# Perceiver layer on one core: the opening by row tile, a sixth key projection in the first block, and the first pair's sums taken from PSUM

## The reference

```python
x = x + xattn(layernorm(x), ctx, Wq, bq, Wk, bk, Wv, bv, Wo, bo)   # 16 heads of 32
x = x + attn(layernorm(x), ...)                                     # self attention, top 128
x = x + ffn(layernorm(x), ...)                                      # 8 experts, top 2

def xattn(q_in, kv, ...):
    q, k, v = heads(q_in @ Wq.T + bq), heads(kv @ Wk.T + bk), heads(kv @ Wv.T + bv)
    return merge(softmax(q @ k.T * 32**-0.5) @ v) @ Wo.T + bo
```

## Time and profile before

| | |
|---|---|
| median of 3 runs | 1579.67 us (1578.26 to 1581.8) |
| span of the profiled execution, first to last instruction | 1576.5 us |
| median less span | 3.2 us |
| time of the profiled execution itself | not recorded beside the three runs; only its span is |
| PE busy | 1508.9 us, 96% of the span |
| DVE, ACT, POOL busy | 79%, 65%, 26% |
| mean granted TensorE clock | 0.981 of full speed |
| PE busy in the first of 40 slices | 6 tenths |
| block 1 | to about 46.9 us |
| block 2 | 46.9 to about 564 us |

### The profile page before, as it was taken

The page is one execution under the profiler, slowest core; times in us unless marked ns, Lnnn a source line. Parts: engine busy times, 40 slices in busy tenths (PEclk is TensorE's granted clock), DMA queues, the critical chain, the costliest instruction groups (busy, mean ns, idle before and its releaser), DMA issues. The chain is left out here.

```text
span 1576.5 us, 23638 instructions
## 1 busy us (share of the span) xinstructions
PE 1508.9 (96%) x8658; PEld 869.0 (55%) x8658; DVE 1240.5 (79%) x1876; ACT 1021.3 (65%) x1343; POOL 411.2 (26%) x225
## 2 busy tenths in 40 slices
PE   6899999999999999999999999999999965999998
PEld 4566666666666554444443444444445732799995
DVE  6877676776767869999998999999876878476664
ACT  3466666666666768888888888888726941244441
POOL 5564545636447010502100400100004420100002
PEclk9999999999999999999999999999999987899999
DMA  6354444444444455456646444545247045399994
GB/s 234 131 189 141 174 174 142 179 153 167 165 157 160 126 142 129 120 129 189 158 114 153 114 127 114 127 114 128 61 54 161 2 159 223 127 340 349 360 333 140
DMA packets 119777, 254.57 MB, mean 161 GB/s; under 512 B 10152, under 2 KB 26536, under 8 KB 115184
## 3 DMA queue, kind: packets, MB, share of 16 engines
q1 hardware_dynamic: 117632, 248.35, 51.1%
q0 software_dynamic: 1408, 4.46, 0.9%
q10 hardware_dynamic: 624, 0.27, 0.1%
HBM read 182.26 MB, written 61.34 MB: 155 GB/s over the span
## 5 line engine op out<-in xcount | busy, mean ns | idle before, releaser
L800 ACT ACTIVATE att_pr<-b_sc 128x1024 f32<-128x1024 f32 x512 | 479.9, 1037 | 82.9 <-PE b_sc L700 82.2
L850 DVE TENSOR_TENSOR att_tot<-att_tot,att_pr 128x2048 f32<-128x2048 f32 x184 | 427.3, 2322 | 21.6 <-ACT att_pr L800 3.4
L519 DVE CUSTOM_DVE_ANT_0 ctx_size<-ctx_tot,ctx_size 128x512 f32<-128x512 f32 x512 | 333.0, 688 | 127.2 <-PE ctx_tot L430 124.1
L481 ACT ACTIVATE ctx_size<-ctx_dif 128x1024 f32<-128x1024 f32 x256 | 262.5, 1025 | 120.0 <-PE ctx_dif L430 120.0
L700 PE MATMUL b_sc<-g_stacks,att_kst 98*128 98x512 f32 x1024 | 298.5, 422 | 1.9 <-DMA att_kst<-keys_scratch 1.7
L700 PEld LDWEIGHTS b_sc<-g_stacks,att_kst 98*128 98x128 f32 x1024 | 174.7, 189 | 192.2 <-ACT att_pr L800 143.2
L714 PE MATMUL b_o<-att_pr,att_val 128*32 128x512 f32 x2048 | 258.4, 602 | 0.9 <-issue 0.9
L430 PE MATMUL ctx_dif<-ctx_k_dif,f_q_hi 32*128 32x512 f32 x512 | 128.2, 497 | 5.8 <-DVE ctx_best L519 4.5
L430 PE MATMUL ctx_tot<-ctx_k_sum,f_q_hi 32*128 32x512 f32 x512 | 127.8, 497 | 0.0
L86 PE MATMUL f_proj<-f_wv_hi,g_stacks 128*128 128x512 f32 x320 | 120.5, 420 | 0.0
L86 PE MATMUL f_proj<-g_stacks,f_wk_hi 128*128 128x512 f32 x352 | 119.4, 420 | 0.3 <-DVE f_k_lo L211 0.3
(11 more groups left out here) (314 smaller groups left out, 2177.2 us busy)
## 6 DMA issues: line engine op xcount, KB each, us to landing
m_w<-in_W SPq DMA_DIRECT2D x30, 2048.0 KB, 10.1
att_kst<-keys_scratch SPq DMA_DIRECT2D x192, 256.0 KB, 4.0
f_raw<-in_ctx SPq DMA_DIRECT2D x32, 1024.0 KB, 6.0
keys_scratch<-f_k_hi SPq DMA_DIRECT2D x32, 512.0 KB, 2.8
keys_scratch<-f_k_lo SPq DMA_DIRECT2D x32, 512.0 KB, 3.2
values_scratch<-ctx_v SPq DMA_DIRECT2D x32, 512.0 KB, 3.4
att_val<-values_scratch SPq DMA_DIRECT2D x64, 256.0 KB, 2.7
rows_scratch<-mix_blank SPq DMA_DIRECT2D x1, 3840.0 KB, 24.1
```

The source lines that it names most:

```text
L481: act.activation(size[:, i % ABS, :], dif[:, :], ACT.Abs).then_inc(s_size, 1)
L519: dve.tensor_tensor_reduce(out=size[:, i % ABS, r * CH:(r + 1) * CH], in0=tot[i % 2][:, r * CH:(r + 1) * CH], in1=size[:, i % ABS, r * CH: ...
L800: act.activation(pr[:, T % SLOTS, 2 * s:2 * s + 2, :], sc[(2 * T + s) % PAIRS][:, :].rearrange("p (j q) -> p j q", j=2), ACT.Exp, scale=SC ...
L850: dve.tensor_tensor(tot[b % 2][:, :, :], so_far, pr[:, T % SLOTS, :, :], ALU.add).then_inc(s_add, 1)
```

## The change

Block 1: x arrives in four DMAs, tiles 0 and 2 issued by SP ahead of the weights and 1 and 3 by ACT ahead of the biases, each with its own semaphore. DVE aggregates tile t-1 behind the statistics of tile t. PE makes 12 products with the identity as soon as that exists, then transposes tile by tile as each tile of h is there (all four columns of one tile into one bank), and ACT copies a bank to a strided quarter of `hT`. At the end PE makes output 5 in place of the ten `keep_warm` matmuls, once `k_lo` of output 3 is done.

Block 2: output 5 is gone from PE's list. `first_pair` now computes (bank + bias) - k_hi[0] and (bank + bias) + k_hi[0] from the PSUM bank that holds the chunk 1 keys, and it stands ahead of the `k_lo` of its output.

```diff
-            sp.dma_start(c.x[:, :, :], c.dram["x"].rearrange("(t p) d -> p t d", p=P)).then_inc(x_in, 16)
+            for t in range(0, NT, 2):
+                sp.dma_start(c.x[:, t, :], c.dram["x"][P * t:P * t + P, :]).then_inc(x_in[t], 16)
...
+            for t in range(1, NT, 2):
+                act.dma_start(c.x[:, t, :], c.dram["x"][P * t:P * t + P, :]).then_inc(x_in[t], 16)
...
-            for k in range(DC):
-                act.wait_ge(s_tp, k + 1)
-                act.activation(hT[:, k, :], tp[k % 2][:, :], ACT.Copy).then_inc(s_hT, 1)
+            for t in range(NT):
+                act.wait_ge(s_tp, t + 1)
+                act.activation(hT[:, :, t * P:(t + 1) * P], tp[t % 2][:, :].rearrange("p (k q) -> p k q", k=DC),
+                               ACT.Copy).then_inc(s_hT, 1)
...
-            pe.wait_ge(s_h, NT)
-            for k in range(DC):
-                if k >= 2:
-                    pe.wait_ge(s_hT, k - 1)
-                for t in range(NT):
-                    mm = pe.transpose(tp[k % 2][:, t * P:(t + 1) * P], h[:, t, k * P:(k + 1) * P], c.ident[:, :])
+            keep_warm(pe, tp[0][:, 0:P], c.ident[:, :], c.ident[:, :], 12)
+            for t in range(NT):
+                pe.wait_ge(s_h, t + 1)
+                if t >= 2:
+                    pe.wait_ge(s_hT, t - 1)
+                for k in range(DC):
+                    mm = pe.transpose(tp[t % 2][:, k * P:(k + 1) * P], h[:, t, k * P:(k + 1) * P], c.ident[:, :])
                 mm.then_inc(s_tp, 1)
...
-            keep_warm(pe, tp[0][:, :], c.wk_hi[:, 0, 0:P], c.wk_hi[:, 0, :], 10)
+            pe.wait_ge(c.k_lo_done, G)
+            split_product(pe, c.proj[1][:, :], [(c.wk_hi[:, k, P:2 * P], c.wk_lo[:, k, P:2 * P]) for k in range(DC)],
+                          [(c.hi[1][:, k, :], c.lo[1][:, k, :]) for k in range(DC)]).then_inc(c.s_out, 1)
...
-    for t in range(NT):
-        dve.bn_stats(stats[:, t, :], x[:, t, :]).then_inc(s_stats, 1)
-    for t in range(NT):
-        dve.wait_ge(s_stats, t + 1)
-        dve.bn_aggr(mv[:, t, :], stats[:, t, :]).then_inc(s_stats, 1)
+    for t in range(NT + 1):
+        if t < NT:
+            dve.wait_ge(x_in[t], 16)
+            dve.bn_stats(stats[:, t, :], x[:, t, :]).then_inc(s_stats, 1)
+        if t:
+            dve.wait_ge(s_stats, max(2 * t - 2, 1) if t < NT else 2 * NT - 1)
+            dve.bn_aggr(mv[:, t - 1, :], stats[:, t - 1, :]).then_inc(s_stats, 1)
...
-            project(FIRST - 1, 0, WHOLE)
             pe.wait_ge(s_pair0, 2)
...
+                    if n == 1:
+                        first_pair(at)
                     dve.wait_ge(k_hi_done, count("k", o + 1))
                     dve.scalar_tensor_tensor(out=k_lo[:, at, :], in0=proj[o % 2][:, :], scalar=c.bk[:, at:at + 1],
                                              in1=f32(k_hi[n % 2][:, at, :]), op0=ALU.add, op1=ALU.subtract).then_inc(k_lo_done, 1)
-                    if n == 1:
-                        first_pair(at)
 
             def first_pair(at):
-                even, odd = f32(k_hi[0][:, at, :]), f32(k_hi[1][:, at, :])
-                dve.tensor_tensor(k_dif[0][:, at, :], even, odd, ALU.subtract).then_inc(s_pair0, 1)
-                dve.tensor_tensor(k_sum[0][:, at, :], even, odd, ALU.add).then_inc(s_pair0, 1)
+
+                o = KT + at
+                dve.wait_ge(k_hi_done, o + 1)
+                for out, op in ((k_dif, ALU.subtract), (k_sum, ALU.add)):
+                    dve.scalar_tensor_tensor(out=out[0][:, at, :], in0=proj[o % 2][:, :], scalar=c.bk[:, at:at + 1],
+                                             in1=f32(k_hi[0][:, at, :]), op0=ALU.add, op1=op).then_inc(s_pair0, 1)
```

More of the change, by code:

```diff
@@ L132, in prepare @@
         qp = [pb(f"qp{i}", [P, N]) for i in range(2)]
-        x_in, wq_in, wk_in, wv_in, small_in = (sem(n) for n in ("x_in", "wq_in", "wk_in", "wv_in", "small_in"))
+        x_in = [sem(f"x_in{t}") for t in range(NT)]
+        wq_in, wk_in, wv_in, small_in = (sem(n) for n in ("wq_in", "wk_in", "wv_in", "small_in"))
         s_const, s_ident = sem("const"), sem("ident")
@@ L198, in _ @@
         def _(dve):
-            dve.wait_ge(x_in, 16)
-            layer_norm(dve, c.x, h, stats, mv, std, rstd, s_stats, s_var, s_std, s_rstd, s_h)
+            layer_norm(dve, c.x, x_in, h, stats, mv, std, rstd, s_stats, s_var, s_std, s_rstd, s_h)
             dve.wait_ge(s_whi, 1)
@@ L249, in _, with layer_norm @@
                           [(c.hi[1][:, k, :], c.lo[1][:, k, :]) for k in range(DC)]).then_inc(c.s_out, 1)
-            keep_warm(pe, tp[0][:, :], c.wk_hi[:, 0, 0:P], c.wk_hi[:, 0, :], 10)
-def layer_norm(dve, x, h, stats, mv, std, rstd, s_stats, s_var, s_std, s_rstd, s_h):
-    for t in range(NT):
-        dve.bn_stats(stats[:, t, :], x[:, t, :]).then_inc(s_stats, 1)
-    for t in range(NT):
-        dve.wait_ge(s_stats, t + 1)
-        dve.bn_aggr(mv[:, t, :], stats[:, t, :]).then_inc(s_stats, 1)
+            pe.wait_ge(c.k_lo_done, G)
+            split_product(pe, c.proj[1][:, :], [(c.wk_hi[:, k, P:2 * P], c.wk_lo[:, k, P:2 * P]) for k in range(DC)],
+                          [(c.hi[1][:, k, :], c.lo[1][:, k, :]) for k in range(DC)]).then_inc(c.s_out, 1)
+def layer_norm(dve, x, x_in, h, stats, mv, std, rstd, s_stats, s_var, s_std, s_rstd, s_h):
+    for t in range(NT + 1):
[5 more added lines that the diff above has]
+            dve.bn_aggr(mv[:, t - 1, :], stats[:, t - 1, :]).then_inc(s_stats, 1)
     dve.wait_ge(s_stats, 2 * NT)
```

## The result

| | before | after |
|---|---|---|
| first comparison, median of 4 runs each | 1580.37 us (1578.26 to 1581.8) | 1570.04 us (1569.18 to 1570.76) |
| later comparison, median of 17 and of 12 runs | 1578.09 us (1573.5 to 1583.18) | 1571.98 us (1567.59 to 1574.31) |
| profiled execution, span | 1576.5 us | 1568.3 us |
| first scores of block 2, step 0, step 9 (start) | 49.98, 51.60, 77.41 | 50.74, 52.35, 72.96 |
| last products out of `k_dif` in block 2 (start) | 560.37 | 552.37 |

The ratio of the first comparison is 0.9939 (95% interval 0.9927 to 0.9952), of the later one 0.9961 (0.9946 to 0.9975). So the kernel is faster, by 10.3 us in the one and 6.1 us in the other, where 5.3 were forecast. The forecast of 1574.4 is 4.4 us above the first median.

What follows compares the result with a forecast made beforehand. PE bounds the kernel, busy 96% of the span. Terms: 1.7 + 0.45 us later, 1.58 + 5.9 earlier, net 5.3 off the 1576.5 span; 1571.2 plus 3.2 to the median gives 1574.4 us, range 1570.5 to 1578.2.

Steps and rivals of the forecast that it cites:

- step 0: Block 2, follows the first scores by an unchanged dependence on ACT, 1.62 us behind them, at 52.17.
- step 9: Block 2, the ruler for the steady pace: start at 72.1 against 77.41, 5.3 us earlier.
- The opening: Block 1 by row tile: queries start 3.8 us earlier, but DVE and POOL alternate; 0.3 us at most, booked 0.
- the third key projection: Block 1, PE waits for `k_lo` of output 0: start stays at 35.87, wait grows from 0.30 to about 4.1 us.
- Block 2 opened: Start of block 2: 46.93 plus 0.45 for output 5 in block 1 and 1.7 for half clock, 49.08.
- the first scores: Block 2, waiting only for the two `first_pair` instructions: 1.47 us behind block 2's start, at 50.55.
- The new sums: `first_pair` in block 2: 0.67 us each whatever POOL does; rival that POOL holds them: 1578.6, chance 0.06.
- Behind the start of the third key projection: Block 1: one half-clock stretch after PE's wait of 4.1 us, +1.7 us, bounds 0 and 3.4.
- the clock doesn't fall: Rival: no half clock in one or both booked places, 1.7 or 3.4 us lower, 1572.7 or 1571.0; chance 0.17.
- Behind the first scores: Block 2: one half-clock stretch after PE's gaps of some 1.8 and 1.1 us, +1.7 us, bounds 0 and 3.4.
- the prediction's reading of it: Block 2's start: its two short gaps wouldn't lower the clock, the time 1.7 us lower, 1572.7; doubted, no own chance.
- 2.02 us a step: Block 2's steady pace: PE is full there, so everything behind moves by as much as the steady pace comes earlier.

## Why the prediction was right, and where its sizes were off

**Held, by its own steps.** The opening is worth nothing by itself: the third key projection, booked at 35.87, started between 35.6 and 36.4 in every trace in which POOL's low part of the value weights stood ahead of it, with the new opening and with the old. What is next there was DVE behind POOL, and taking POOL away moved the opening of block 2 by 3.5 us against the trace without half clock at that place and by 5.6 us against the one with it. Block 2 opened at 49.27 (booked 49.08), the first scores came 1.47 us behind (booked 1.47), step 0 another 1.61 (booked 1.62). The new sums were 0.75 us each beside POOL, the old ones beside POOL still 2.4 to 4.4 in the two kernels that kept them, and with the new sums no maximum was late. Here the Trainium skill bears on it ("SBUF — State Buffer", section "Who interferes with whom"): a DVE instruction with two inputs in SBUF contends with one of GpSimd that reads SBUF; one with at most one input there doesn't, unless it runs in a mode that uses both ports, as casts can. This case's traces agree: 4.09 us for L509 (the opening alone) against 0.75 for L513 (the full change), both beside a POOL L100, and 4.82 us for the cast L210 beside L172.

**The half clock, place by place.** Behind the start of the third key projection it cost the booked 1.7. That the size came out is in part luck: the wait ahead of it was 1.88 us, not 4.1, because PE made the queries partly at half clock and ended them later; in the other traces of the same kernel the wait was 3.35 (one 3.4 us stretch) and 0.22 us (none). So in these three traces this term is 0 or 1.7, by how fast the queries were, and it is one with the rival "the clock doesn't fall". Behind the first scores the stretch was 3.4 us in one trace of the changed kernel and 6.8 in two: 1.5 to 2.5 us, where I booked 1.7 with 3.4 as the bound. Filling the second pair of gaps, and cutting the first wait to 1.29 us, removed both. In the traces of the three kernels with block 2's gaps filled no half clock stands there; in the ten others it does. That shows that it comes from PE's gaps, short ones of 1.8 and 1.1 us included. The Trainium skill ("TensorE: Matmul & The Clock Gate", section "HAM oscillation — how this bites in real kernels") describes long waits for DMA; the prediction's reading of it, that short gaps cost nothing, does not hold here. The trace without the identity products is the plain case, with one stretch and no wait over 1.8 us.

**The size.** At equal pace the change is worth, at the last products out of `k_dif`, 5.8 us and 6.5 us (554.57 and 553.85 against 560.37), and 4.4 us at step 9 in the first trace: around the 5.3 forecast. In the medians of 17 and 12 runs it is 6.1. The first comparison said 10.3. Of its two traces 3.55 us were the pace that each execution drew, and its few runs of before lay high: 1580.37, where three samples of 30, 7 and 17 runs had 1578.47, 1579.13 and 1578.09. Read by the prediction's own list, 1570.04 would have been its rival without any half clock (1571.0), and the trace, with half clock in both places, refutes that: the number alone would have pointed to a wrong cause.

**The step that failed.** That behind step 9 it goes on at 2.02 us a step, so that everything there moves by as much, is an assumption that the trace of one execution can't bear: 3.55 of the 8.2 us of span came from there. What I gave as half a us of spread was several us: the kernel before alone ran from 1571.5 to 1583.2 us. Also missing was the half clock during the queries, 2.3 us of PE's time, which was hidden here only because PE would have waited anyway. And the opening's own 3.8 us were booked too high: 3.57, 3.14 and 2.67 us in the three traces.

**Open.** What settles the pace of an execution isn't known. It isn't the order of the instructions, since the same program drew two values. From the last products out of `k_dif` to the end it took from 1010.7 to 1018.4 us. Most of that goes with a half-clock stretch near 570 us: the six traces with 6.8 us of it took 1015.9 to 1018.4, the one with 3.4 us 1014.7, the six with none 1010.7 to 1014.5. Both traces of the kernel before and all three of the changed one have it, so it doesn't enter their difference. The traces of the new sums alone and of the three filled kernels don't, and their spans are some 4 us shorter there; whether the edits have to do with it is not shown, and I didn't try what brings it. Nor is it known why the queries of the new opening ran partly at half pace in five of eight traces (15.68 to 16.45 us; 13.97 in the other three; in four of the five the granted clock shows it), and in none of the five with the old opening.

## What to carry to other kernels

A DVE instruction that reads two SBUF operands beside a busy GpSimd is worth rewriting to take one operand from PSUM where the value still is: here that alone gave what the whole change gave, within the spread of the runs, while freeing PE earlier gave nothing until GpSimd's work was moved behind the DVE work that PE waits for. Before you move a start forward, name the last instruction ahead of the next wait that doesn't move; here it stood on another engine. And before a difference of 0.3% is believed, put the durations of one untouched instruction beside each other in both traces.

## What the runs showed of the hardware that I had not expected

- At full granted clock the same 128x128 by 128x512 matmul had one of four patterns through all of block 2: 388 ns in three traces, 397 in seven, 397 and 398 in one, 387 to 396 in two, which made 32.10, 32.37, 32.43 and 32.59 us for 16 steps. Over the 13 such sets of block 2 the ends are some 6.4 us apart (13 times 0.49).
- Gaps of PE of 1.8 and 1.1 us with two matmuls between were followed by 3.4 or 6.8 us of half clock, while single waits of 1.34 and 1.29 us with PE busy on both sides were followed by none.
- A cast of DVE from SBUF to SBUF, with one input only, was held by POOL as well: 0.42 us alone, 4.82 us beside L172. The earlier trace rows already had it, at 4.78 us.
- One place near 570 us ran 6.8 us at half clock in six of thirteen traces, 3.4 us in one and not at all in six, and the part of the kernel behind block 2, the same in all of them, was some 4 us longer with it.
